# Gated cross-attention with a routed feed-forward: loads ordered by need, four small query groups, score chunks of 128 keys, normalisation spread over slots, the last two tiles multiplied by all experts

## The chip, the core and the metric

The kernel runs on one NeuronCore of a Trainium2 chip. The metric is the device time of one launch in microseconds (us), the median of three runs. The engines work beside each other: TensorE (PE) multiplies, VectorE (DVE) and ScalarE (ACT) read its PSUM results, GpSimd (POOL) works on SBUF only, SyncE (SP) starts transfers (DMA). They meet at semaphores. Every engine runs its own instructions strictly in the order in which they are written.

## The reference

```python
# x (8, 112, 256), ctx (8, 375, 192), 16 heads of 16
x = x + tanh(g_xattn) * xattn(layernorm(x), ctx, ctx, Wq, bq, Wk, bk, Wv, bv, Wo, bo)
x = x + tanh(g_ffn) * ffn(layernorm(x), wg, W, b)

def xattn(...):   # q = query @ Wq + bq, k = ctx @ Wk + bk, v = ctx @ Wv + bv
    return (softmax(q k^T / 4) v) @ Wo + bo          # for each of the 16 heads

def ffn(x, wg, W, b):                                # all 896 tokens, 8 experts
    probs = softmax(x @ wg); idx = argmax(probs)
    mask = one_hot(idx); loc = cumsum(mask) - mask   # place of a token with its expert
    mask = mask * (loc < 112)                        # C = 896 / 8
    return probs[idx] * (W[idx] @ x + b[idx])        # the expert's product, weighted
```

A token beyond its expert's 112 places gets nothing from the feed-forward. The kernel's gathered table has 112 rows for each expert (`CAP`).

## The kernel before

A tile is one batch element: 112 queries by 375 keys. Queries and keys are split into three bf16 parts, laid out by small transfers (`lay_q`, `lay_k`, issued by SP) in six rows per head dimension, so that one bf16 matmul per head gives a score in nearly full precision.

The work is written as a pipeline of slots. A loop over `s` runs on every engine, and each step of a tile has an offset: `at(s, OFFSET, n)` says which tile `b` does that step in slot `s`. A tile begins every 12 slots (`TURN`), so that each slot holds work of up to five tiles. The steps of a tile are, with their first offset in the code before:

- K steps (`project_k`, offsets -16 to -14) multiply keys; ACT makes `k_hi` and a copy (`k_copy`) of each half at -14 and -12; POOL splits the halves (`k_split`, three instructions) at -13 and -11; SP lays them out at -7.
- `scores` and `take_max` (0 to 11): one matmul per head into one of two PSUM banks (`sc`), and one DVE maximum over the 375 keys. A bank is used again when its maximum is taken.
- `split_max` (13) on POOL makes three bf16 parts of the 16 maxima, `turn_max` (14) on PE turns them, ACT copies them (`mrows`), SP lays them out (14 to 15, `MROW_AT`), so that the second score product subtracts the maximum.
- `scores_T` (17 to 28): the scores once more, transposed, four heads and one of three chunks of 125 keys each slot (`stp`); ACT takes the exponential (`prob`); `probs_v` (18 to 29) multiplies by the values, four heads in four strips of 32 columns.
- V steps (`project_v`, 12 to 16) make the values of the tile.
- `normalise_pv` (30) on DVE: transpose out of PSUM, reciprocal, product, transpose back; `through_wo` (31) on PE; `add_x` (32) on DVE with the statistics of the second layer norm.
- `rstd_2` and `normalise_2` (33) on POOL (the last two tiles' `normalise_2` on DVE), `turn_xn2` (35), `logits` (36).

So offset 35 of one tile, offset 11 of the tile two further and offset -13 of the tile four further are the same slot (35 = 12 x 3 - 1, and so on): each slot has a number from 0 to 11 in its turn of 12, and it is this number that counts for what meets on an engine. Within a slot the order is that of the loop's body. On POOL it is `split_max`, `k_split`, and then the second layer norm.

The first stage works on queries by groups (`QG`: tile 0, tiles 1 to 4, tiles 5 to 7). After the last slot comes the feed-forward. Tiles 0 to 6 are scattered by expert into a table in HBM (`scatter`, POOL), loaded again as eight blocks (`xin`), multiplied by their expert (`product`) and scattered to the output. Tile 7 is not scattered: it is multiplied by all eight experts (`dense`, 16 matmuls of 512 columns), and DVE adds the products by the token's share.

Of the kernel before, what the change touches and what calls it, by code (L numbers as in the profile page):

```python
# [22 lines left out]
NCH = 3  # L23
KN = NK // NCH
# [11 lines left out]
KR = 3  # L36
# [18 lines left out]
FIRST, LAST = -4, TURN * (B - 1) + LG_AT  # L55


QG = ((0, 1), (1, 5), (5, 8))

R0, R1, R2 = (0, 6), (6, 7), (7, 8)  # L60
ROUTE0_AT, PLACE0_AT, ASSIGN0_AT = 97, 98, 99
ROUTE1_AT, PLACE1_AT, ASSIGN1_AT = 109, 110, 111
SCAT0_AT = (100, 101, 102, 106, 107, 108)
# [20 lines left out]
def v_block(c, h):  # L84

    return (h, 24 + h, 16 + h if h < 8 else 32 + h)[c]


def build(nc, x, ctx, gx, gf, wq, bq, wk, bk, wv, bv, wo, bo, wg, wT, be, out):
# [3 lines left out]
    with ExitStack() as stack:  # L93
# [10 lines left out]
        bq_sb = sb("bq_sb", [128, 2])  # L104
        bk_sb = sb("bk_sb", [128, 2])
        bv_sb = sb("bv_sb", [128, 2])
# [7 lines left out]
        half = sb("half", [NQ, B])  # L114
# [21 lines left out]

        st1 = sb("st1", [NQ, B, 6])
        mv1 = sb("mv1", [NQ, B, 2])
        ve1 = sb("ve1", [NQ, B])
# [4 lines left out]
        k6_flat = sb("k6", [128, KR, H * NK], BF16)  # L144
        k6 = k6_flat[:, :, :].rearrange("p r (h n) -> p r h n", n=NK)
# [5 lines left out]
        prob = sb("prob", [128, 3, 4 * NQ])  # L151
        pvT = sb("pvT", [128, NQ * G])
# [6 lines left out]
        ve2 = sb("ve2", [NQ, B])  # L159
# [30 lines left out]
        s_x = [sem(f"x_of_group_{g}_loaded") for g in range(3)]  # L190
# [21 lines left out]
        s_qzero = [sem(f"zeros_in_q_{g}_ready") for g in range(3)]  # L212
# [5 lines left out]
        s_stat = sem("variance_ready")  # L218
        s_rstd = sem("rstd_ready")
# [8 lines left out]
        s_qlaid = [sem(f"q_rows_of_group_{g}_laid") for g in range(3)]  # L228
# [21 lines left out]
        s_x1 = sem("x1_ready")  # L250
        s_stat2 = sem("variance_2_ready")
# [12 lines left out]
        s_scat = sem("tokens_scattered")  # L264
        s_xin = [sem(f"expert_{e}_loaded") for e in range(E)]
# [8 lines left out]
        s_dense = sem("all_experts_product_in_psum")  # L274
        s_counted = sem("places_of_last_tile_taken")
# [4 lines left out]
        s_last = sem("last_tile_ready")  # L280
# [34 lines left out]
        def _(sp):  # L315
# [13 lines left out]
            def lay_k(b):  # L329
# [15 lines left out]
            sp.dma_start(wk_sb[:, :, :], wk).then_inc(s_wk, 16)  # L345
            load_ctx(0, 0, 1)
            sp.dma_start(x_sb[:, 1:5, :], x[:, 1:5, :]).then_inc(s_x[1], 16)
            load_ctx(1, 1, 2)
            sp.dma_start(x_sb[:, 5:B, :], x[:, 5:B, :]).then_inc(s_x[2], 16)
            lay_k(0)  # L350
            lay_q(0)
            for s in range(FIRST, LAST + 1):
                if s == 1:
                    lay_q(1)
                    load_ctx(2, 2, 5)
# [21 lines left out]
                if s == 93:  # L377
                    sp.wait_ge(s_x1, 6)
# [787 lines left out]
```

## Time and profile before

| what | value |
|---|---|
| runs | 225.04, 225.27, 226.06 us; median 225.27 |
| profiled execution | 226.61 us, of which the span from the first to the last instruction is 224.8 |
| PE busy | 184.9 us, 82% of the span, 1692 matmuls |
| DVE / ACT / POOL busy | 123.7 / 91.5 / 94.3 us |
| chain that ended last | PE 66%, DVE 13%, DMA 8%, POOL 5% |
| mean granted TensorE clock | 0.922 |
| HBM | read 10.03 MB, written 5.29 MB |

In the profile PE is a matmul's time and PEld a weight load's. The chain of waits is followed back from the last instruction: each piece is what released the one behind it, so pieces of PE there are times for which PE alone decided. Three stages can be told apart in it: 0 to 54.6 us, until the first transposed scores; 54.6 to 189.2 us, eight turns of 12 slots, some 18 us each where all steps are present; and 189.2 to 224.8 us, the rest of tile 7 and the experts.

### The profile page before, as it was taken

How to read it: one execution, taken by the hardware profiler on the slowest of the kernel's cores; microseconds unless marked ns; L12 is line 12 of the kernel's file. 1: busy time of each engine (PE TensorE's matmuls, PEld its weight loads, DVE VectorE, ACT ScalarE, POOL GpSimd, SP SyncE). 2: the span in 40 equal slices, each digit the busy share in tenths (PEclk: the TensorE clock that was granted, in tenths of full speed). 3: DMA queues.
4: the chain of work that ended last, by engine and by line, in shares of the span. 5: the costliest groups of instructions: out<-in, count | busy, mean ns of one | idle time of the engine just before them, and what ended most of it. 6: DMA issues, size and time to landing. Idle time of an engine off the chain costs nothing.

```text
span 224.8 us, 4335 instructions
## 1 busy us (share of the span) xinstructions
PE 184.9 (82%) x1692; PEld 111.7 (50%) x1692; DVE 123.7 (55%) x292; ACT 91.5 (41%) x200; POOL 94.3 (42%) x145
## 2 busy tenths in 40 slices
PE   0866869743999899899899989989989896479990
PEld 0342426412556466557556646646656563257640
DVE  7037465563454855754764675485585436254651
ACT  0262243231374365456527527544636654021200
POOL 5632639779245056038037235413022553103730
PEclk9999599995699999999999999999999998556998
DMA  6968049999940910840660490180351233560110
GB/s 187 264 156 169 0 107 291 226 238 294 291 139 16 224 65 5 191 109 3 142 162 0 100 203 3 40 171 0 94 146 57 69 113 116 155 175 28 57 51 20
DMA packets 17660, 27.40 MB, mean 122 GB/s; under 512 B 4007, under 2 KB 12817, under 8 KB 17272
## 3 DMA queue, kind: packets, MB, share of 16 engines
q1 hardware_dynamic: 15176, 23.82, 41.6%
q0 software_dynamic: 944, 2.28, 3.3%
q10 hardware_dynamic: 1520, 1.03, 1.9%
q8 instruction: 13, 0.21, 0.4%
q14 instruction: 7, 0.06, 0.1%
HBM read 10.03 MB, written 5.29 MB: 68 GB/s over the span
## 4 chain that ended last, share of the span: by engine, by line
PE 66%; DVE 13%; DMA 8%; POOL 5%; ACT 2%; issue 2%; ACTq 1%; SPq 1%; DVEq 0%
PE stp L476 14%; PE pv L491 12%; PE sc L465 8%; PE misc L522 4%; PE stp L407 4%; DMA bv_sb<-in_bv 4%; DVE nmax L809 4%; PE pj L423 3%; PE pj L439 3%; PE misc L580 2%; DVE pvT L816 2%; DMA k<-parts_k 2%; DMA q<-mrows 2%; PE pj L444 2%; PE pv L580 2%
## 5 line engine op out<-in xcount | busy, mean ns | idle before, releaser
L809 DVE TENSOR_REDUCE nmax<-sc 112x1 f32<-112x375 f32 x128 | 68.2, 543 | 54.6 <-PE sc L465 53.8
L733 ACT ACTIVATE prob<-stp 125x448 f32<-125x448 f32 x96 | 52.2, 544 | 61.2 <-PE stp L476 60.8
L465 PE MATMUL sc<-k,q 128*112 128x375 bf16 x128 | 41.8, 343 | 9.1 <-DVE nmax L809 6.7
L476 PE MATMUL stp<-q,k 128*125 128x112 bf16 x384 | 42.8, 236 | 3.2 <-DMA q<-mrows 3.2
L491 PE MATMUL pv<-prob,v_sb 125*32 125x112 f32 x768 | 38.7, 273 | 2.1 <-issue 1.3
L476 PEld LDWEIGHTS stp<-q,k 128*125 128x125 bf16 x384 | 30.3, 140 | 20.1 <-issue 16.5
L491 PEld LDWEIGHTS pv<-prob,v_sb 125*32 125x32 f32 x768 | 15.4, 108 | 23.6 <-ACT prob L733 10.1
L1000 POOL TENSOR_SCALAR ve<-mv 112x1 f32<-112x1 f32 x8 | 1.9, 233 | 57.4 <-DVE mv L838 57.4
L465 PEld LDWEIGHTS sc<-k,q 128*112 128x112 bf16 x128 | 17.2, 135 | 16.4 <-DVE nmax L809 11.4
L423 PE MATMUL pj<-ctx_sb,wk_sb 128*128 128x375 f32 x32 | 15.4, 580 | 7.8 <-DMA ctx_sb<-in_ctx 7.8
L1017 POOL TENSOR_TENSOR kf<-kf,parts_k 128x375 f32<-128x375 f32 x14 | 12.6, 899 | 19.1 <-ACT kf L677 19.1
L1011 POOL TENSOR_TENSOR parts_k<-kf,parts_k 128x375 bf16<-128x375 f32 x16 | 13.9, 875 | 5.1 <-ACT parts_k L665 4.0
L407 PE MATMUL stp<-early,wq_sb 128*128 128x112 f32 (+2 forms) x24 | 10.9, 615 | 2.8 <-ACT early L665 2.8
L671 ACT ACTIVATE parts_k<-pj,bk_sb 128x375 bf16<-128x375 f32 x16 | 9.0, 572 | 10.1 <-PE pj L428 8.2
L1117 POOL DMA_INDIRECT out<-res,ctx_sb x8 | 7.8, 974 | 12.4 <-DVE res L968 11.2
L423 PEld LDWEIGHTS pj<-ctx_sb,wk_sb 128*128 128x128 f32 x32 | 6.9, 235 | 9.6 <-issue 7.9
L522 PE MATMUL misc<-wo_sb,onorm 128*112 128x256 f32 x32 | 9.3, 418 | 2.3 <-DVE onorm L826 2.3
L1040 POOL DMA_INDIRECT slots<-rows,slot x7 | 7.1, 1016 | 8.2 <-DVE slot L888 6.8
L439 PE MATMUL pj<-wv_sb,ctx_sb 128*125 128x256 f32 x32 | 9.8, 389 | 0.7 <-ACT kf L677 0.7
L407 PEld LDWEIGHTS stp<-early,wq_sb 128*128 128x128 f32 x24 | 5.7, 282 | 6.5 <-issue 4.9
L428 PE MATMUL pj<-ctx_sb,wk_sb 64*128 64x375 f32 x32 | 8.3, 596 | 0.0
L677 ACT ACTIVATE kf<-pj,bk_sb 128x375 f32<-128x375 f32 x14 | 8.0, 572 | 0.0
(125 smaller groups left out, 240.7 us busy)
## 6 DMA issues: line engine op xcount, KB each, us to landing
k<-parts_k SPq DMA_DIRECT2D x48, 187.5 KB, 3.8
ctx_sb<-in_ctx SPq DMA_DIRECT2D x2, 1125.0 KB, 7.6
early<-in_wT SPq DMA_DIRECT2D x8, 256.0 KB, 4.3
slots<-empty SPq DMA_DIRECT2D x8, 224.9 KB, 4.6
ctx_sb<-slots SPq DMA_DIRECT2D x8, 224.9 KB, 4.5
q<-parts_q SPq DMA_DIRECT2D x6, 224.0 KB, 3.7
q<-parts_q SPq DMA_DIRECT2D x6, 168.0 KB, 3.7
k<-in_be SPq DMA_DIRECT2D x1, 896.0 KB, 5.1
```

The costliest lines, as they stand in the source:

```text
L407: mm = pe.matmul(stp[m][:, 0:(hi - lo) * NQ], wq_sb[:, c, m * 128:(m + 1) * 128], xnT[:, c, lo * NQ:hi * NQ], start=(c == 0), stop=(c == 1))
L423: pe.matmul(pj[n][:, 0:NK], wk_sb[:, 0, n * 128:(n + 1) * 128], ctx_sb[:, b, 0, :], start=True, stop=False)
L439: pe.matmul(pj[n][0:KN, 0:D], keys(n, slice(0, 128), 0), wv_sb[:, 0, :], start=True, stop=False)
L465: pe.matmul(sc[h % 2][0:NQ, 0:NK], q_heads(b)[:, h, :], k6[:, b % KR, h, :], start=True, stop=True).then_inc(s_sc, 1)
L476: mm = pe.matmul(stp[n % 2][0:KN, j * NQ:(j + 1) * NQ], k6[:, b % KR, h, c * KN:(c + 1) * KN], q_heads(b)[:, h, :], start=True, stop=True)
L491: mm = pe.matmul(pv[32 * j:32 * j + 32, g * NQ:(g + 1) * NQ], v_sb[0:KN, b % VR, v_block(c, 4 * g + j), :], prob[0:KN, n % 3, j * NQ:(j + ...
L522: mm = pe.matmul(misc[0:NQ, 0:D], onorm[:, g, :], wo_sb[:, g, :], start=(g == 0), stop=(g == 1))
L671: nc.scalar.activation(parts_k[:, b % 2, 0, m, :], pj[m][:, 0:NK], ACT.Identity, bias=bk_sb[:, m:m + 1]).then_inc(s_khi, 1)
L733: nc.scalar.activation(prob[0:KN, n % 3, :], stp[n % 2][0:KN, 0:4 * NQ], ACT.Exp, scale=SCALE).then_inc(s_p, 1)
L809: nc.vector.tensor_reduce(nmax[:, b % 2, h:h + 1], sc[h % 2][0:NQ, 0:NK], axis=AX.X, op=ALU.max, negate=True).then_inc(s_max, 1)
L1011: nc.gpsimd.tensor_tensor(parts_k[:, b % 2, 2, m, :], kf[:, b % 2, m, :], parts_k[:, b % 2, 1, m, :], ALU.subtract).then_inc(s_klo, 1)
L1017: nc.gpsimd.tensor_tensor(kf[:, b % 2, m, :], kf[:, b % 2, m, :], parts_k[:, b % 2, 0, m, :], ALU.subtract).then_inc(s_krest, 1)
```

## The change

- Loads: keys, values, biases (one packed array) and weights are asked for in the order of their use and from other queues; the context of tiles 2 to 4 is asked for by ACT, far earlier. A first activation loads the table ahead of its use.
- Query groups: tile 0, tiles 1 and 2, tiles 3 to 5, tiles 6 and 7. The K steps of tile 1 move ahead of the slots, and POOL's constants behind the splits of tile 1 and of group 1. The slots begin at 0.
- The score chunks have 128, 128 and 119 keys. `scores_T` loads 128 columns of weights for every chunk; for the last these go past the tile's end by 9 columns, whose results are not read.
- `normalise_pv` is cut into `turn_pv`, `divide` and `turn_back` in slots 30, 31 and 32, with the maxima of these slots between them. `through_wo` moves to 33, `add_x` to 34, `rstd_2` and `normalise_2` to 35, `turn_xn2` to 37, `logits` to 38. `split_max` moves forward to 12, `turn_max` to 13. `turn_xn2` shares a PSUM bank with the maxima and now waits for `mrows` of the tile two further.
- Tiles 6 and 7 are both multiplied by all experts (`dense(t, p)`), and six tiles are scattered. The dense products of tile 6 are written between the last steps of tile 7 on PE.

```diff
-V_EARLY = -10
-SPLITMAX_AT, MAXT_AT, MROW_AT = 13, 14, 15
+V_EARLY = -11
+SPLITMAX_AT, MAXT_AT, MROW_AT = 12, 13, 14
 T_AT, PV_AT = 17, 18
-NORM_AT, WO_AT, ADD_AT = 30, 31, 32
-LN_AT, X2T_AT, LG_AT = 33, 35, 36
+NORM_AT, WO_AT, ADD_AT = (30, 31, 32), 33, 34
+LN_AT, X2T_AT, LG_AT = 35, 37, 38
-QG = ((0, 1), (1, 5), (5, 8))
+QG = ((0, 1), (1, 3), (3, 6), (6, 8))
...
-                    mm = pe.matmul(stp[n % 2][0:KN, j * NQ:(j + 1) * NQ],
-                                   k6[:, b % KR, h, c * KN:(c + 1) * KN], q_heads(b)[:, h, :],
+                    k0 = h * NK + CHUNKS[c][0]
+                    mm = pe.matmul(stp[n % 2][:, j * NQ:(j + 1) * NQ],
+                                   k6_flat[:, b % KR, k0:k0 + 128], q_heads(b)[:, h, :],
...
             def turn_xn2(b):
                 pe.wait_ge(s_xn2, b + 1)
+                pe.wait_ge(s_mrows, min(b + 3, B))
...
+            turn_share(0)
+            dense(0, 0)
+            through_wo(B - 1)
+            choose_bias(0)
+            dense(0, 1)
+            turn_xn2(B - 1)
             turn_xin(0)
-            places(2, *R2)
-            for e in range(1, E):
+            logits(B - 1)
+            dense(0, 2)
+            places(2, B - 1, B)
+            dense(0, 3)
+            turn_xin(1)
...
+            for p in range(4):
+                dense(1, p)
...
-                if found := at(s, NORM_AT, 1):
-                    normalise_pv(found[0])
+                if found := at(s, NORM_AT[0], 1):
+                    turn_pv(found[0])
+                if found := at(s, NORM_AT[1], 1):
+                    divide(found[0])
+                if found := at(s, NORM_AT[2], 1):
+                    turn_back(found[0])
...
+            for m in range(2):
+                k_split(1, m)
+            rstd(3)
+            for m in range(2):
+                q_lo(1, m)
+            ones_in_k(2)
+            zeros_in_q(2)
+            zeros_in_q(3)
```

The tables of offsets do not show what meets on an engine. On POOL, in a turn with all steps (`kf` and `parts_k` are the key split, `ve`, `rs` and `rows` the second layer norm, `mparts` the parts of the maxima), before:

```order
L1000 TENSOR_SCALAR ve<-mv 112x1
L1001 TENSOR_TENSOR rs<-ve,half 112x1
L1006 TENSOR_SCALAR rows<-rows,mv,rs 112x256
L1017 TENSOR_TENSOR kf<-kf,parts_k 128x375
L1020 CAST parts_k<-kf 128x375
L1011 TENSOR_TENSOR parts_k<-kf,parts_k 128x375
L1033 CAST mparts<-nmax 112x16
L1034 TENSOR_TENSOR mrest<-nmax,mparts 112x16
```

The same place on POOL in the changed kernel:

```order
L1105 TENSOR_TENSOR parts_k<-kf,parts_k 128x375
L1094 TENSOR_SCALAR ve<-mv 112x1
L1095 TENSOR_TENSOR rs<-ve,half 112x1
L1100 TENSOR_SCALAR rows<-rows,mv,rs 112x256
L1127 CAST mparts<-nmax 112x16
L1128 TENSOR_TENSOR mrest<-nmax,mparts 112x16
```

The layer norm (three instructions) stood ahead of the first key split, and now stands between it and the parts of the maxima.

On PE, from the last K step of a tile (its second half, `pj<-ctx_sb,wk_sb` twice) to the turn of the maxima (`misc<-ident_b,mparts`), before:

```order
L428 MATMUL pj<-ctx_sb,wk_sb 128x375 x2
L491 MATMUL pv<-prob,v_sb 32x112 x4
...
L439 MATMUL pj<-wv_sb,ctx_sb 125x256
L491 MATMUL pv<-prob,v_sb 32x112 x4
L476 MATMUL stp<-q,k 125x112 x4
L465 MATMUL sc<-k,q 112x375
L444 MATMUL pj<-wv_sb,ctx_sb 125x256 x2
L515 MATMUL misc<-ident_b,mparts 48x112
L491 MATMUL pv<-prob,v_sb 32x112 x4
```

and in the changed kernel, the end of the same stretch:

```order
L449 MATMUL pj<-wv_sb,ctx_sb 128x256
L528 MATMUL misc<-ident_b,mparts 48x112
L546 MATMUL misc<-ident,rows 128x112 x2
L503 MATMUL pv<-prob,v_sb 32x112 x4
L487 MATMUL stp<-q,k 128x112 x4
L475 MATMUL sc<-k,q 112x375
L454 MATMUL pj<-wv_sb,ctx_sb 128x256 x2
```

The turn of the maxima has moved ahead of a `pv` product, a `stp` group, a score and the two V products of 256 columns, and the turn of the normalised rows (`misc<-ident,rows`) now stands right behind it.

On DVE, the normalisation and the maxima around it, before:

```order
L809 TENSOR_REDUCE nmax<-sc 112x1 x13
L816 STREAM_TRANSPOSE pvT<-pv 128x448
L818 RECIPROCAL rden<-pvT 128x14
L819 TENSOR_TENSOR onT<-pvT,rden 128x2x7x16
L826 STREAM_TRANSPOSE onorm<-onT 128x224
L809 TENSOR_REDUCE nmax<-sc 112x1 x3
```

and in the changed kernel:

```order
L881 STREAM_TRANSPOSE pvT<-pv 128x448
L883 RECIPROCAL rden<-pvT 128x14
L874 TENSOR_REDUCE nmax<-sc 112x1 x2
L886 TENSOR_TENSOR onT<-pvT,rden 128x2x7x16
L874 TENSOR_REDUCE nmax<-sc 112x1
L895 STREAM_TRANSPOSE onorm<-onT 128x224
L874 TENSOR_REDUCE nmax<-sc 112x1 x3
```

Three maxima have moved in between the four instructions of the normalisation.

## Rows read from the trace of the kernel before

**Rows 1.** The page: busy time and share of each engine.

```profile
PE 184.9 (82%) x1692; PEld 111.7 (50%) x1692; DVE 123.7 (55%) x292; ACT 91.5 (41%) x200; POOL 94.3 (42%) x145
```

**Rows 2.** Windows, one turn: length, busy by engine, PEclk, DMA share, GB/s.

```profile
94.00:112.00 18.00, 17.01 (x196) 10.47 (x195) 10.99 (x24) 9.76 (x21) 7.26 (x13) 1.00 0.40 93
```

**Rows 3.** Chain of waits, one turn: start us, us, what.

```profile
109.21 0.55 DVE nmax L809
...
111.95 0.37 PE sc L465
...
117.18 0.83 PE pj L428 x4
118.01 0.33 PE pv L491 x8
118.34 0.37 PE stp L476 x4
118.70 0.16 PE sc L465
...
119.92 0.43 PE pj L439 x2
```

**Rows 4.** Timeline, same turn: start us, us, engine, line, operation, [idle before].

```profile
114.47 0.23 POOL L1000 TENSOR_SCALAR ve<-mv 112x1 f32<-112x1 f32 x1 [7.74 <-DVE mv L838]
115.47 1.23 POOL L1006 TENSOR_SCALAR rows<-rows,mv,rs 112x256 f32<-112x256 f32 x1
...
118.51 0.57 ACT L677 ACTIVATE kf<-pj,bk_sb 128x375 f32<-128x375 f32 x1
119.16 0.90 POOL L1017 TENSOR_TENSOR kf<-kf,parts_k 128x375 f32<-128x375 f32 x1 [2.46 <-ACT kf L677]
121.50 0.20 POOL L1033 CAST mparts<-nmax 112x16 bf16<-112x16 f32 x1
122.34 0.22 POOL L1036 TENSOR_TENSOR mparts<-mrest,mparts 112x16 bf16<-112x16 f32 x1
123.52 0.23 PE L515 MATMUL misc<-ident_b,mparts 112*48 112x112 bf16 x1
123.79 0.26 ACT L665 ACTIVATE mrows<-misc 48x112 bf16<-48x112 f32 x1 [0.41 <-PE misc L515]
```

**Rows 5.** Timeline, weight loads of one group of four transposed score matmuls.

```profile
181.66 0.31 PEld L476 LDWEIGHTS stp<-q,k 128*125 128x125 bf16 x4 [0.17 <-issue]
```

**Rows 6.** Chain of waits, first stage.

```profile
23.26 6.17 PE stp L407 x8
29.63 1.00 DVE nmax L809 x2
...
40.07 0.87 POOL kf L1017
...
42.74 4.59 DMA k<-parts_k
...
50.06 4.51 DMA q<-mrows
```

**Rows 7.** Windows of PE (last numbers: PEclk, DMA share, GB/s), and chain.

```profile
56.00:60.00 4.00, 4.00 (x31) 0.52 1.07 260
...
57.33 0.61 PE stp L476 x4
...
58.79 0.61 PE stp L476 x4
```

**Rows 8.** Chain of waits, last stage; last row from the timeline.

```profile
189.30 0.66 DVE pvT L816
...
191.16 2.06 PE misc L522 x4
...
212.09 1.72 PE pj L560 x4
...
220.89 0.32 SPq L387 DMA_DIRECT2D out<-last  x1
```

More of the change, by code:

```diff
@@ L433, in keys @@
                 def keys(c, rows_in, part):
-                    return ctx_sb[rows_in, b, part, c * KN:(c + 1) * KN]
+                    k0, kn = CHUNKS[c]
+                    return ctx_sb[rows_in, b, part, k0:k0 + kn]
+                half = D // 2
+                kn = CHUNKS[2][1]
                 if n < 2:
@@ L438, in project_v @@
                     pe.wait_ge(s_kf, 2 * (newest - 1) + n + 1)
-                    pe.matmul(pj[n][0:KN, 0:D], keys(n, slice(0, 128), 0), wv_sb[:, 0, :],
+                    pe.matmul(pj[n][:, half:half + D], keys(n, slice(0, 128), 0), wv_sb[:, 0, :],
                               start=True, stop=False)
@@ L443, in project_v @@
                         rows_in = slice(c * REST, (c + 1) * REST)
-                        pe.matmul(pj[c][0:KN, 0:D], keys(c, rows_in, 1), wv_sb[rows_in, 1, :],
+                        pe.matmul(pj[c][:, half:half + D], keys(c, rows_in, 1), wv_sb[rows_in, 1, :],
                                   start=False, stop=True, tile_position=(c * REST, 0))
@@ L447, in project_v @@
                     for c in range(2):
-                        pe.matmul(pj[c][0:KN, D:D + 128], keys(2, slice(0, 128), 0),
-                                  wv_sb[:, 0, c * 128:(c + 1) * 128], start=True, stop=False)
+                        pe.matmul(pj[c][0:kn, 0:half], keys(2, slice(0, 128), 0),
+                                  wv_sb[:, 0, c * half:(c + 1) * half], start=True, stop=False)
                 if n == 4:
@@ L452, in project_v @@
                         rows_in = slice(c * REST, (c + 1) * REST)
-                        pe.matmul(pj[c][0:KN, D:D + 128], keys(2, rows_in, 1),
-                                  wv_sb[rows_in, 1, c * 128:(c + 1) * 128], start=False, stop=True,
+                        pe.matmul(pj[c][0:kn, 0:half], keys(2, rows_in, 1),
+                                  wv_sb[rows_in, 1, c * half:(c + 1) * half], start=False, stop=True,
                                   tile_position=(c * REST, 0)).then_inc(s_v, 1)
@@ L970, in _ @@
                                                ALU.mult, ALU.add).then_inc(s_res, 1)
-            dve.wait_ge(s_share, 1)
-            dve.wait_ge(s_beT, 1)
-            link(nc.vector.tensor_tensor(last[:, :], pv[0:NQ, 0:D], rows[:, b, X1:X1 + D], ALU.add))
-            banks = (pj[0], pj[1], stp[0], stp[1])
-            for e in range(E):
-                if e % 2 == 0:
-                    dve.wait_ge(s_dense, e // 2 + 1)
-                ins = nc.vector.scalar_tensor_tensor(
-                    last[:, :], banks[e // 2][0:NQ, (e % 2) * D:(e % 2 + 1) * D], share[:, e:e + 1],
-                    last[:, :], ALU.mult, ALU.add)
-                if e < E - 1:
-                    link(ins)
-                else:
-                    ins.then_inc(s_last, 1)
+                if e == 3:
+                    take_bias(1)
+            for p in range(4):
+                add_dense(1, p)
         @block.gpsimd
@@ L1079, in more_constants @@
                     .then_inc(s_eno, 1)
[L1081 to L1085 removed]
+            for s in range(END):
                 if found := at(s, SPLITMAX_AT, 1):
```

473 lines of the change are left out of this document (268 added, 205 removed).

## The prediction

> **What bounds the kernel now.** I read the page first: PE is busy for 184.9 of 224.8 us, the next engine for 124 [rows 1]. Then the windows of one turn of 12 slots: 17.01 of 18.00 us are PE's, at the full clock of 2.4 GHz, while DVE has 11, ACT 10 and POOL 7 [rows 2]. So in the middle of the program PE decides, and a cut in its work or in its waits counts in full. Then the chain of waits in such a turn: the only pieces there that aren't PE's lie between 109.21 and 111.95 us, where PE waits for DVE, which does a whole normalisation ahead of a maximum [rows 3]. Last I looked at what is late without deciding: POOL finishes the parts of the maxima at 122.56, and PE asks for them at 123.52, 0.96 us later [rows 4]. The changed order is read against this margin.
>
> The sum goes by the profiled execution, 226.61 us with a span of 224.8; the median of the runs is 225.27. The difference that I forecast is added to the median.
>
> **Loads, groups, first stage.** Before, the first maximum starts at 29.63, behind a 6.17 us product for a group of four tiles [rows 6]; with two tiles it is half. In the new order DVE does the statistics of tiles 6 and 7 and two query rests ahead of the first maximum, and these wait for the smaller product; stepping the new order through with the old durations gives about 27.2. The keys of tile 1 were split late, at 40.07, behind POOL's constants, and landed at 47.33 [rows 6]; now they are there before they are asked for. What is late next is the turn of tile 0's maxima. The twelve slots between took 17.7 us (29.63 to 47.33), some 3.4 of it waits that go (keys of tile 1, context of tile 2), and get about 1 of new query work: 15. The key split of tile 2 and the parts of the maxima follow on POOL, so that the max rows are asked for near 47, not 50.06. Their transfer took 4.51 beside a load of 1.1 MB [rows 6], which is over by then; with 3.4 the transposed scores start at 50.3, not 54.6. Taken: **-4.3**; bounds 0 (another wait in the place of that for the keys) and -7.3 (the whole of 47.33 to 54.6).
>
> **Normalisation.** Before, the score behind it starts at 111.95. Now `pv` needs only the first transpose, done at about 110.35; with a `pv` product (0.33) and a `stp` group (0.37) the score stands at 111.06, and it then takes 0.16, not 0.37 [rows 3]. That is 1.05 a turn, for six turns with scores beside it, and 0.5 for tile 6: **-6.8**. Bounds 0 and -9.4: of the 2.74 us up to 111.95, two `stp` groups, two scores and a `pv` product are work, 1.39, and the other 1.35 would go in seven turns. Moving `through_wo` by two slots keeps its wait at nothing.
>
> **The turn of the maxima.** Here the change costs. Two moves meet. PE asks a slot earlier, and on POOL the layer norm now stands between the key split and the parts of the maxima, because offsets 35 and -13 share a slot and the loop writes the split first; `split_max` at 12 comes behind both. From the end of the last K step on PE (118.01): ACT's copy is done at 119.08, POOL's split runs from 119.16 to 121.50, 2.34; the layer norm takes 2.23 (114.47 to 116.70); the parts 1.06 (121.50 to 122.56) [rows 3, 4]. In sum 1.15 + 2.34 + 2.23 + 1.06 + 0.05 = 6.83 us. PE's own work in that time is 0.33; then 0.37 + 0.16 + 0.33; then 0.37 + 0.43 + 2 x 0.16 + 0.33; then 0.37 + 0.16 + 0.43: 3.60 [rows 3], or 3.3 with the shorter groups below. PE waits 3.5 us, and nothing passes it. Behind `turn_max` stands `turn_xn2`, which now waits until ACT has copied the maxima: 123.52 to 124.05 [rows 4], 0.4 beyond the matmul itself. That is 3.9 a turn where K steps and layer norm both occur: slots 35, 47, 59, 71, four turns, 15.6. The turn before has the key split alone (4.6 - 3.3 = 1.3), the two behind the layer norm alone (0.7 and 1.2 by the same steps, from `add_x`). Together **+18.8**; bounds +8 (were the layer norm free) and +22.
>
> **Chunks of 128 keys.** 96 groups of four. A group takes 0.37 [rows 3]; its four loads of 125 bf16 columns take 0.31 with about 0.057 between starts [rows 5]. A score of 375 columns takes 0.16 behind a load of 112 columns, so 112 columns stream in 0.048, and four in 0.19. So the load, not the stream, sets the group. No row shows a bf16 load of 128 columns. Bounds: no gain, or a loss of 3 columns in 125 (+0.01 a group), and 0.18 gained, when only the stream is left. The third chunk moves no result: the same count of columns. I take the middle, 0.09, as nothing in the rows favours an end: 96 x 0.09 = **-8.6**.
>
> The Trainium skill has a rule here ("TensorE: Matmul & The Clock Gate", section on Fast Weight Load): a non-fp32 load of exactly 128 columns is split in four parallel chunks, four times as fast in theory and about twice as measured. With loads at half their time the group would fall by some 0.07 to 0.09, with a quarter by up to the bound; no row of this trace shows it, since its 128-column loads are all fp32.
>
> **The clock.** A wait of 3.5 us is long enough for the clock to matter. Before, PE stands for most of the 4.51 us in which the max rows land (until 54.6) [rows 6]; in 56 to 60 it is granted 0.52, and a slot takes 1.46 (57.33 to 58.79) [rows 7], where the same slot takes 0.86 at the full clock [rows 3]. 0.52 is nearly all of the window at the 1.2 GHz level, so the low level lasts some 5.3 us past the restart there and costs 5.3 x (1 - 0.86 / 1.46) = 2.2. With part of it inside the wait I take 1.8 for each of the four long waits: **+7.2**; bounds 0 and +12 (the short ones too).
>
> **The end.** From the last transposed product to the end it is 35.5 us now. There DVE's normalisation runs from 189.30, and the product through `wo` takes 2.06, at half the clock [rows 8]. Now two of four parts of tile 6's dense product, 1.72 each [rows 8], lie in the waits of tile 7's chain, and six scatters instead of seven bring the expert blocks earlier. Stepping through the new order at the full clock, tile 7's logits come at 6.5, the first expert product at 11.7, the eighth at 20.4, tile 7's dense products at 27.3, the last issue at 28.4, and 3.9 to the end [the last issue is at 220.89, rows 8]: 32.4, 3.1 less. If the clock falls as before, a dense part of 3.4 us stands ahead of `wo`: +3. Half of that: **-1.6**; bounds -4 and +2.
>
> Sum: -4.3 - 6.8 + 18.8 - 8.6 + 7.2 - 1.6 = **+4.7**. The profiled execution would take 231.3, the median 230.0.
>
> **Rivals.**
> (a) *The loads nearly vanish.* By the same rule at its fullest a group takes 0.19: 8.6 more is gained, and 1.4 of it lost again in longer waits (POOL's path doesn't shrink): 222.8, faster. For: four loads fill 0.31 of 0.37. Against: the first load of each group stays exposed behind `pv`. 0.12.
> (b) *The clock holds.* PE works densely around the waits, and each may be too short. Then 230.0 - 7.2 = 222.8, faster. For: it held through 1.35 us of idling a turn [rows 2, 3]. Against: the idling ahead of 54.6 is of the same length, and there the level was low. 0.15.
> (c) *128 columns load as 125 do.* +8.6 and the waits shorter by 1.4: 237.2, slower. 0.08.
> (d) *The first stage gains nothing*, since transfers or POOL's constants hold the max rows: 234.3. For: the DMA engines are full in much of that stage. 0.12.
> (e) *The POOL path is shorter than I say*, because PE's slots are longer than I add up (the waits that I left out stand on its side), so that the wait is 1.5 us, not 3.5: 4 x 2.0 less, 222. 0.05.
> My forecast, wait of 3 to 4 us and low clock behind it: 0.48, alone 226 to 235.
>
> Within 0.5% (224.1 to 226.4) no difference can be told from none. From the cases: faster, most of (a), (b), (e) and a sliver of the forecast, 0.27; same 0.10; slower 0.63. Range 220.5 to 237.
>
> **What would show it.** In the changed profile the trace must have PE waiting for POOL's `mparts` for about 3.5 us ahead of L528 in four turns, POOL going from `rows` L1100 straight to `mparts`, and turns of 20 to 22 us there, against under 17 where neither K steps nor layer norm meet. The 128-column loads show their price in the length of a `stp` group: 0.28 by my sum, 0.19 by (a), 0.38 by (c). PEclk shows 5s behind each wait, or not (b). The first transposed scores near 50.3, and the last stage near 33 to 34 us. The forecast is wrong if these waits are under 2 us, or if PE keeps its clock.

## The result

| | before | changed |
|---|---|---|
| runs, median (lowest to highest) | 225.36 us (225.04 to 226.06) | 256.62 us (256.1 to 258.94) |
| span of the profiled execution | 224.8 | 254.8 |
| mean granted TensorE clock | 0.922 | 0.886 |

The ratio is 1.140, 95% interval 1.133 to 1.148. Some executions of a kernel take over 1.5% longer than its fastest, and the ratios here leave these out. Forecast were 230.0 us and a range up to 237: the direction was right, the size far off. In a later comparison the changed kernel took 260.04 us (258.61 to 261.44) beside 228.48, ratio 1.143 (1.131 to 1.155):

> The changed kernel once more, beside the others on the same chip: 1.12 to 1.145 of the kernel before.

Three points in both traces place the 30.0 us. The first transposed scores start at 59.56, not 54.61: +5.0. From there to the last `pvT` transpose it is 160.8 us (to 220.38), not 134.7 (to 189.30): +26.1. The last stage has 34.4, not 35.5: -1.1.

One part of this differs from execution to execution. In the profiled one of the later comparison (span 258.4) tile 7's slots, from 207 on, take 17.4 us, not 13.4, and the rest is within 0.5 us of the above.

### The profile page after: what moved, and what is told of

Same layout as the page of the kernel before. It is cut to its first block, busy times and chain, and to the rows that moved or that the text cites. A ratio compares the mean times of both kernels' runs of the same rounds, so it can differ in the third digit from the quotient of the medians.

```text
span 254.8 us, 4453 instructions
## 1 busy us (share of the span) xinstructions
PE 196.3 (77%) x1719; PEld 113.2 (44%) x1719; DVE 137.6 (54%) x301; ACT 92.5 (36%) x208; POOL 96.0 (38%) x164
## 4 chain that ended last, share of the span: by engine, by line
PE 50%; POOL 19%; DVE 17%; issue 5%; ACT 4%; DMA 3%; POOLq 0%; DVEq 0%
PE stp L487 7%; PE pv L503 7%; PE sc L475 7%; DVE early L854 4%; DVE nmax L874 4%; PE pj L583 3%; PE pj L454 3%; PE pj L430 3%; POOL rows L1100 3%; POOL kf L1111 3%; POOL parts_k L1105 3%; PE misc L538 2%; PE misc L555 2%; PE pj L435 2%; PE pj L458 2%
## 5 line engine op out<-in xcount | busy, mean ns | idle before, releaser
L790 ACT ACTIVATE prob<-stp 128x448 f32<-128x448 f32 (+1 forms) x96 | 52.0, 544 | 54.5 <-PE stp L487 53.4
L503 PE MATMUL pv<-prob,v_sb 128*32 128x112 f32 (+1 forms) x768 | 41.0, 289 | 1.9 <-issue 1.4
L487 PE MATMUL stp<-q,k 128*128 128x112 bf16 x384 | 38.8, 229 | 0.2 <-DMA q<-mrows 0.2
L487 PEld LDWEIGHTS stp<-q,k 128*128 128x128 bf16 x384 | 22.3, 104 | 18.9 <-issue 18.3
L503 PEld LDWEIGHTS pv<-prob,v_sb 128*32 128x32 f32 (+1 forms) x768 | 16.1, 113 | 24.2 <-issue 9.4
L854 DVE TENSOR_SCALAR early<-x_sb,mv,rs 112x256 f32<-112x256 f32 x8 | 13.5, 1728 | 5.0 <-POOL rs L1089 5.0
L528 PE MATMUL misc<-ident_b,mparts 112*48 112x112 bf16 x8 | 1.9, 240 | 17.4 <-POOL mparts L1130 17.4
L583 PE MATMUL pj<-early,x2T 128*112 128x512 f32 x24 | 13.1, 682 | 0.5 <-DVE q L981 0.5
L713 ACT ACTIVATE parts_k<-pj,bqkv_sb 128x375 bf16<-128x375 f32 x16 | 9.0, 572 | 6.6 <-PE pj L435 6.6
L449 PE MATMUL pj<-wv_sb,ctx_sb 128*128 128x256 f32 x32 | 11.1, 431 | 0.1
L1119 POOL TENSOR_TENSOR parts_q<-early,parts_q 128x224 bf16<-128x224 f32 (+2 forms) x8 | 5.6, 715 | 14.7 <-ACT parts_q L707 14.7
L528 PEld LDWEIGHTS misc<-ident_b,mparts 112*48 112x48 bf16 x8 | 0.8, 101 | 20.5 <-POOL mparts L1130 20.5
```

Source lines behind the costliest of these rows:

```text
L449: pe.matmul(pj[n][:, half:half + D], keys(n, slice(0, 128), 0), wv_sb[:, 0, :], start=True, stop=False)
L487: mm = pe.matmul(stp[n % 2][:, j * NQ:(j + 1) * NQ], k6_flat[:, b % KR, k0:k0 + 128], q_heads(b)[:, h, :], start=True, stop=True)
L503: mm = pe.matmul(pv[32 * j:32 * j + 32, g * NQ:(g + 1) * NQ], v_sb[0:kn, b % VR, v_block(c, 4 * g + j), :], prob[0:kn, n % 3, j * NQ:(j + ...
L583: mm = pe.matmul(bank[0:NQ, 0:2 * D], x2T[:, (GATHERED + t) % 2, c, :], wT_sb[:, 2 * p:2 * p + 2, c, :], start=(c == 0), stop=(c == 1))
L713: nc.scalar.activation(parts_k[:, b % 2, 0, m, :], pj[m][:, 0:NK], ACT.Identity, bias=bk_sb[:, m:m + 1]).then_inc(s_khi, 1)
L790: nc.scalar.activation(prob[0:kn, n % 3, :], stp[n % 2][0:kn, 0:4 * NQ], ACT.Exp, scale=SCALE).then_inc(s_p, 1)
```

## The profile after

The page of the changed kernel, the row that answers to [rows 1], and the granted clock in 40 slices:

```profile
PE 196.3 (77%) x1719; PEld 113.2 (44%) x1719; DVE 137.6 (54%) x301; ACT 92.5 (36%) x208; POOL 96.0 (38%) x164
PEclk9999558995999965997699679959999999589999
```

PE is busy for 11 us more. The dense products of tile 6 are new work, 4 x 1.72 us [rows 8], and the shorter `stp` groups take about as much away, so most of the 11 is slower work. The clock row says where: between slices 15 and 27 (89 to 172 us) it dips once a turn.

**The first stage.** Timeline of the changed kernel around the first maximum:

```profile
25.86 1.98 POOL L1119 TENSOR_TENSOR parts_q<-early,parts_q 128x224 bf16<-128x224 f32 x2
25.92 8.61 DVE L854 TENSOR_SCALAR early<-x_sb,mv,rs 112x256 f32<-112x256 f32 x2 [1.48 <-POOL rs L1089]
27.78 2.67 POOL L1147 MEMSET k<- 128x1000 f32 x3
30.40 3.99 POOL L1152 MEMSET q<- 128x896 f32 x5
34.33 1.69 POOL L1172 MEMSET v_sb<- 128x1536 f32 x1
34.63 0.99 DVE L874 TENSOR_REDUCE nmax<-sc 112x1 f32<-112x375 f32 x2
35.22 0.56 PE L475 MATMUL sc<-k,q 128*112 128x375 bf16 x1 [7.64 <-DVE nmax L874]
```

Two instructions of DVE, the normalisation of tiles 6 and 7, take 8.61 us. Apart, the first takes 1.45 beside POOL's `q_lo`, the second 7.23: it starts before the memset of `k` and ends with the last memset of `q`. The first maximum, forecast at 27.2, starts at 34.63, and PE stands 7.64 us for it. DVE's own idle time ahead of the pair is 1.48; the rest is in the length of the instruction, so it is held off while it runs.

**A turn of 12 slots.** Timeline of one turn, which answers to [rows 4]:

```profile
135.42 0.90 POOL L1111 TENSOR_TENSOR kf<-kf,parts_k 128x375 f32<-128x375 f32 x1 [16.10 <-ACT kf L719]
136.96 0.85 POOL L1105 TENSOR_TENSOR parts_k<-kf,parts_k 128x375 bf16<-128x375 f32 x1
138.76 1.23 POOL L1100 TENSOR_SCALAR rows<-rows,mv,rs 112x256 f32<-112x256 f32 x1
140.79 0.22 POOL L1130 TENSOR_TENSOR mparts<-mrest,mparts 112x16 bf16<-112x16 f32 x1
141.06 0.23 PE L528 MATMUL misc<-ident_b,mparts 112*48 112x112 bf16 x1 [3.10 <-POOL mparts L1130]
141.33 0.26 ACT L707 ACTIVATE mrows<-misc 48x112 bf16<-48x112 f32 x1 [3.66 <-PE misc L528]
141.73 0.38 PE L546 MATMUL misc<-ident,rows 112*128 112x112 f32 x2 [0.44 <-ACT mrows L707]
```

This is the forecast path, POOL going from the key split through the layer norm to the parts of the maxima, and the forecast wait: 3.10 us, and 3.10 to 3.12 in four turns. Then 0.44 more for ACT's copy. Windows of the same turn (columns as in [rows 2]), of a stretch behind the wait, and of one ahead of its end:

```profile
126.94:150.93 23.99, 20.09 (x197) 11.63 (x195) 10.96 (x24) 9.81 (x22) 7.22 (x13) 0.86 0.30 71
142.34:149.16 6.82, 6.82 (x51) 4.36 (x47) 1.69 (x4) 1.79 (x5) 0.93 (x2) 0.50 0.02 4
136.00:141.00 5.00, 1.94 (x18) 0.79 (x16) 1.54 (x3) 1.67 (x4) 4.43 (x11) 1.00 0.00 0
```

The turn takes 24.0 us, where [rows 2] had 18. PE works 1.94 of the 5 us up to 141 at the full level, and from 142.34 on 6.82 us without a gap at 0.50, 1.2 GHz: its densest work falls where it is slowest. The four turns with K steps and layer norm take 24.7, 24.0, 24.0, 24.0, not 18.16 each: +24.1 of the 26.1 us.

**The last slots.** Timeline, tile 7's slots; the last two rows are PE's wait for the normalised rows of tile 6:

```profile
213.21 0.94 POOL L1134 DMA_INDIRECT slots<-rows,slot  x1 [0.30 <-issue]
214.53 0.57 POOL L1095 TENSOR_TENSOR rs<-ve,half 112x1 f32<-112x1 f32 x1
215.14 0.41 DVE L911 TENSOR_SCALAR rows<-rows,mv,rs 112x256 f32<-112x256 f32 x1 [3.23 <-POOL rs L1095]
215.61 0.41 PE L546 MATMUL misc<-ident,rows 112*128 112x112 f32 x2 [2.30 <-DVE rows L911]
```

Five of six scatters stand ahead of `rstd_2` of tile 6. This wait of 2.30 us is not in the forecast.

The 17.4 us that the same slots take in the later comparison have another reason. There ACT stands for 3.85 us ahead of an exponential, though its input was there at 212.81, and PE stands with it (`remote` and `issue`: the profile shows no instruction that was waited for):

```profile
215.90 0.54 ACT L790 ACTIVATE prob<-stp 119x448 f32<-119x448 f32 x1 [3.85 <-remote]
216.50 0.60 PE L503 MATMUL pv<-prob,v_sb 119*32 119x112 f32 x8 [3.69 <-issue]
```

The profiled executions of e1, e5, e8 and e10 below have the same stop of 3.8 us at this exponential and e2 has one of 2.4; the first one of the changed kernel and those of e3, e6, e9 and e11 have none. What ACT waits for is open. These slots take 13.4 to 17.7 us in all these executions, so turns say more than whole times.

For the last stage, windows of the kernel before and of the changed one, from the last `pvT` to the end:

```profile
189.30:224.80 35.50, 24.18 (x85) 14.91 (x85) 16.65 (x46) 3.74 (x12) 8.75 (x11) 0.74 0.28 81
```

```profile
220.38:254.80 34.42, 28.64 (x104) 15.45 (x104) 20.57 (x55) 3.93 (x13) 8.61 (x10) 0.94 0.27 76
```

PE has 4.5 us more to do, at a better clock; the chain ends with two stretches of `dense` of tile 7, 3.4 us each.

## The experiments

The theory after the comparison: three causes. POOL's memsets hold off DVE's normalise (first stage); the wait of 3.1 us in four turns; and the low clock that it sets off, which costs as much again. The rivals are given with each. Beside these runs the kernel before took 228 us in the median (223.9 to 230.9 over all), so each ratio is to executions of it taken beside that run. `pvT` to `pvT` is a turn.

**e1, order on POOL.**

```diff
+                if found := at(s, LN_AT, 1):
+                    rstd_2(found[0])
+                    if found[0] < GATHERED:
+                        normalise_2(found[0])
                 for m in range(2):
                     if (found := at(s, KSPLIT_AT[m], 1)) and found[0] > 1:
                         k_split(found[0], m)
...
-                if found := at(s, LN_AT, 1):
-                    rstd_2(found[0])
-                    if found[0] < GATHERED:
-                        normalise_2(found[0])
```

> The changed kernel with one edit: on POOL the second layer norm of a slot is written ahead of the key split, as it was before the change. Theory W (PE's wait for the parts of the maxima, and the low clock behind it, are the loss in the middle): the layer norm has its input some 1.7 us before the key split has, so about 2 us leave POOL's path; the wait of 3.1 us ahead of L528 in four turns falls to about 1, the 6.83 us at the low level behind each of them go (3.4 us a turn by half the clock), turns fall from 24.0 to 18.5, and the time from 256.6 to about 235. Theory W2 (the wait matters, the clock falls all the same): only 4 x 2 us, about 248. Rival (the turns are long for a reason that is not this wait): no change, 255 to 258.

Measured: 255.74 us (249.61, 255.27, 256.20 and 256.43) beside 228.3; no ratio is given. In the profiled execution, that of 256.20, the wait at L528 fell from 3.10 to 1.60 in the four turns, and the turns only to 23.70. Windows of one turn of it, and of the stretch behind its wait:

```profile
124.82:148.52 23.70, 21.30 (x197) 12.14 (x195) 10.96 (x24) 9.92 (x22) 7.20 (x13) 0.78 0.32 73
137.79:148.03 10.24, 9.92 (x75) 6.02 (x79) 2.25 (x5) 3.21 (x8) 1.80 (x3) 0.50 0.12 32
```

The low level lasts 10.24 us here, not 6.8, and 1.2 of the 1.5 us won came back as slow work. W, 235 us, is out. In this execution halving the wait bought almost nothing. That can't be said of the one of 249.61 us, which is near W2's 248; its mean clock was 0.881, not 0.851, and it has no trace.

**e8, the wait filled with work.**

```diff
+                if 2 <= b <= 5:
+                    pe.wait_ge(s_x1, b - 1)
+                    for _ in range(7):
+                        pe.matmul(misc[0:NQ, 0:D], wo_sb[:, 0, 0:NQ], wv_sb[:, 0, :], start=True, stop=True)
                 pe.wait_ge(s_mp, b + 1)
```

> The changed kernel as it is, with seven further fp32 products of 256 columns on PE ahead of the turn of the maxima for tiles 2 to 5, written to misc and read by nobody: 14 passes of 0.22 us, 3.08 us, put into the wait of 3.1 us. Nothing else moves; POOL's path is as long as before. Theory K (PE idles, and so the clock falls, and the low clock costs as much as the wait): the clock stays at the full level in these four turns, which fall from 24.0 to 20.6: 256.6 - 4 x 3.4 = 243, though PE does more work. Rival H (the level does not depend on that wait): the products come on top or change nothing, 256 or more, and the level is low for 6.8 us a turn as before.

Measured: 247.79 us (245.9 to 248.35), ratio 1.084 (1.076 to 1.093), where the changed kernel has 1.14. Windows of a turn, and the products in the timeline of the turn ahead of it:

```profile
121.50:142.55 21.05, 20.18 (x211) 12.34 (x209) 10.94 (x24) 9.80 (x22) 7.21 (x13) 1.00 0.33 81
111.28 3.19 PE L523 MATMUL misc<-wv_sb,wo_sb 128*112 128x256 f32 x14
114.56 0.23 PE L532 MATMUL misc<-ident_b,mparts 112*48 112x112 bf16 x1
```

The kernel does seven products more in each of four turns and is 9 to 12 us faster. POOL's path is as before: the turn of the maxima (here L532) starts 14.22 us behind `pvT` in this turn, as in the changed kernel. PE is busy meanwhile (14 passes in 3.19 us), and the level is full from 65.07 to 205.01. Only what stands behind the wait got shorter. So the low level costs 24.0 - 21.05 = 2.9 us a turn, 3.6 in the first of the four: 12.4 in all. Theory K is shown, rival H is out.

**e10, a later turn with the layer norm in the way; e5, both moves undone.**

```diff
-SPLITMAX_AT, MAXT_AT, MROW_AT = 12, 13, 14
+SPLITMAX_AT, MAXT_AT, MROW_AT = 13, 14, 15
-LN_AT, X2T_AT, LG_AT = 35, 37, 38
+LN_AT, X2T_AT, LG_AT = 35, 38, 39
```

> The changed kernel with the parts, the turn and the layout of the maxima at 13, 14, 15 again (turn_xn2 and logits at 38 and 39), but with the layer norm still behind the key split on POOL. Separates the two moves that met: 1.9 us of PE work come ahead of L528, the path on POOL keeps its 2.2 us. PE's wait falls from 3.1 to about 1.2. If a wait of that size still sets off the low level (1.6 us did in e1): turns of 22 to 23.5 and 250 us or so. If the level holds: turns of 24.0 - 1.9 - 3.4 = 18.8 to 19.2, 236 us. Either way the time lies between that of e1 and of e5.

> The changed kernel with the order on POOL of e1_pool_order, and with the parts of the maxima, their turn and their layout at offsets 13, 14, 15 again (turn_xn2 and logits one slot later, 38 and 39). e1 left a wait of 1.6 us, and the low level behind it grew to 10.24 us a turn, so that the turn only fell from 24.0 to 23.7. Theory K (any wait of that length there sets off the low level, and that is what costs): a slot more of PE work (a pv product, a stp group, a score and two V products, 1.9 us) covers the 1.6 us; no wait, full clock, and the turn is that of before, 18.16, less 1.05 for the normalisation and 0.64 for the loads (what the before-kernel with 128-column loads gained a turn): 16.5; the time falls by 4 x 7.2 us to 227 to 230. Rival H (PE's clock falls in these turns for another reason, such as the denser work): turns stay at 22 to 24, time at 250 or more.

Measured: e10 247.47 us (245.88 to 248.07), ratio 1.087 (1.076 to 1.098); e5, with e1's order as well, 233.49 us (232.37 to 234.72), ratio 1.026 (1.019 to 1.034). Windows of the four turns of e10:

```profile
78.09:97.57 19.48, 16.98 (x197) 9.92 (x195) 10.95 (x24) 9.82 (x22) 7.25 (x13) 1.00 0.38 89
97.57:118.59 21.02, 18.52 (x197) 11.16 (x195) 10.95 (x24) 9.81 (x22) 7.25 (x13) 0.92 0.35 81
118.59:141.14 22.55, 20.07 (x196) 11.83 (x194) 11.04 (x25) 10.04 (x22) 7.24 (x13) 0.82 0.38 90
141.14:162.48 21.34, 19.20 (x200) 11.51 (x198) 10.96 (x24) 9.71 (x21) 7.23 (x13) 0.87 0.29 66
```

The wait at L528 is 1.68 to 1.71 us in all four turns (1.2 was expected), and the clock answers differently: no fall in the first turn, 3.41 us at the low level in the second, 10.24 in the third, 3.41 in the fourth. With the same wait the turn costs 19.5, 21.0, 22.5 or 21.3. In e5 the wait is 0.17 to 0.20, the clock is full from 62.67 to 188.97, and the four turns take 17.94 to 17.97. That is K once more, but not the 16.5 expected (nor the 227 to 230 us): e5 has hardly a wait and no low clock there, and gained only 0.2 on the 18.16 of before. With the loads (0.63, e4) and the spread (0.69, e7) it should be 16.84; 1.1 us a turn was still missing (e9).

**e2 and e11, the first stage.** POOL waits until xn is written, ahead of `q_lo` (e2), or behind it (e11):

```diff
             rstd(3)
+            pool.wait_ge(s_xn, B)
             for m in range(2):
                 q_lo(1, m)
             ones_in_k(2)
```

```diff
             for m in range(2):
                 q_lo(1, m)
+            pool.wait_ge(s_xn, B)
             ones_in_k(2)
```

> The changed kernel with one more wait: POOL starts its q_lo of group 1 and its memsets (k, q, v_sb) only when DVE has written all eight tiles of xn. Theory C (DVE's two-input-free SBUF-to-SBUF normalise and POOL's work in SBUF hold each other up: 8.61 us for two instructions at 25.92): the two take about 0.41 us each, the first maximum starts near 27.5 instead of 34.63, and since POOL's constants start 1 us later only, the first transposed scores come about 4 to 7 us earlier than 59.56: 250 to 252. Rival D (the 8.61 us are a wait for something else, such as the loads that land at that time): the two instructions stay near 8 us and POOL's constants come 8 us later: 257 or more.

> The changed kernel with POOL's wait for xn between its q_lo of group 1 and its memsets, not ahead of both. In the changed kernel the first of the pair of DVE's normalise (25.92) took 1.45 us beside q_lo, the second 7.23 us beside the memsets of k and q, and ended with the last of them. Theory C1 (the memsets hold DVE's instruction off, q_lo only slows it): the pair takes some 1.9 us and ends near 27.9, the first maximum comes near 28.2, 0.8 us behind e2's, the first transposed scores near 53.3. Theory C2 (any work of POOL in SBUF that follows without a gap does it): the second instruction starts behind q_lo all the same, and the result is as C1 or up to 0.5 us later. Rival D (something else held DVE until 34.5): the pair still takes over 6 us and the memsets start behind it, at 34 or later. Time of the run by C1: 2 to 5 us below the changed kernel's, ratio 1.12 to 1.135.

Measured: e2 254.86 us (252.73 to 257.7), ratio 1.131 (1.107 to 1.155); e11 253.86 us (253.42 to 254.58), ratio 1.129 (1.117 to 1.140). Timelines of e2 and then of e11:

```profile
25.82 0.73 DVE L854 TENSOR_SCALAR early<-x_sb,mv,rs 112x256 f32<-112x256 f32 x2 [1.49 <-POOL rs L1089]
27.75 2.67 POOL L1147 MEMSET k<- 128x1000 f32 x3
52.48 0.56 PE L487 MATMUL stp<-q,k 128*128 128x112 bf16 x4 [0.31 <-DMA q<-mrows]
```

```profile
25.80 1.30 DVE L854 TENSOR_SCALAR early<-x_sb,mv,rs 112x256 f32<-112x256 f32 x2 [1.48 <-POOL rs L1089]
```

The same two instructions take 0.73 us, or 1.30 beside `q_lo`, not 8.61, and the memsets start no later. The first maximum comes at 27.43 (e11: 28.21), and the first transposed scores at 52.48 (52.79). 7.1 us of the first stage were this. That the memsets held the instruction is shown; D is out. C2, that a run of any other POOL work would do the same, was not separated: in e11 only two `q_lo` instructions follow each other there. The whole time shows less than the trace. For e2 250 to 252 was expected, and both intervals overlap the 1.133 to 1.148 of the changed kernel, so a gain in the whole time, of some 1%, is not clear of noise. In e2 2.9 of the 7.1 us go in tile 7's slots (16.3, not 13.4), where ACT stops for 2.4 us and, from 207.14, the level is low for 13.65 us.

**e3, scatters.**

```diff
-SCAT_AT = (102, 103, 104, 105, 106, 107)
+SCAT_AT = (102, 103, 104, 108, 109, 110)
```

> The changed kernel with three of the six scatters written behind rstd_2 of tile 6 on POOL. Theory T (the scatters of 0.95 us and 1.25 from start to start stand ahead of rstd_2(6), whose input is there at 211.9 and which starts at 214.17, and PE waits 2.3 us for it at L546): rstd_2 starts near 212.2, PE's wait of 2.30 us goes, and the clock may hold at 217.43; the time falls by 2 to 4 us, 253 to 254.5. Rival: the feed-forward waits for the scatters instead (expert blocks land later): no change, or 1 us more.

Measured: 259.47 us (256.77 to 260.5), ratio 1.143 (1.119 to 1.168). PE's wait of 2.30 us at L546 is gone (its weight load waits 0.26), but there is no gain in the time: in this execution the clock fell at 204.98 for 10.24 us, ahead of the place that was changed. That the scatters made the wait is shown, its worth is not; the 253 to 254.5 us expected did not come.

**e4, the kernel before with loads of 128 columns.**

```diff
-        k6_flat = sb("k6", [128, KR, H * NK], BF16)
+        k6_flat = sb("k6", [128, KR, H * NK + 16], BF16)
...
-                    mm = pe.matmul(stp[n % 2][0:KN, j * NQ:(j + 1) * NQ],
-                                   k6[:, b % KR, h, c * KN:(c + 1) * KN], q_heads(b)[:, h, :],
+                    k0 = h * NK + c * KN
+                    mm = pe.matmul(stp[n % 2][:, j * NQ:(j + 1) * NQ],
+                                   k6_flat[:, b % KR, k0:k0 + 128], q_heads(b)[:, h, :],
```

> The kernel before with one edit: each weight load of scores_T takes 128 columns of keys instead of 125, the three further columns give rows of PSUM that nobody reads. This prices the load alone. If a load of 128 bf16 columns is the faster kind: each of 96 groups of four takes 0.28 us or less instead of 0.37, and the time falls by up to 8 us if PE decides in every slot, to 217 to 220; it falls by less where ACT's exponentials (0.54 a slot) or DVE's maxima decide. If it costs as 125 columns do: 225 to 226, no change.

Measured: 222.17 us (221.18 to 222.73), ratio 0.983 (0.968 to 0.998). Timeline of one group (compare [rows 5]) and windows of a turn of e4:

```profile
109.32 0.21 PEld L477 LDWEIGHTS stp<-q,k 128*128 128x128 bf16 x4 [0.17 <-issue]
```

```profile
105.64:123.17 17.53, 16.47 (x197) 9.83 (x195) 11.15 (x25) 9.64 (x22) 7.26 (x13) 1.00 0.43 99
```

Four loads of three columns more take 0.21 us, not 0.31. In the chain a group takes 0.30, not 0.37. The turn falls by 0.63. The Trainium skill ("TensorE: Matmul & The Clock Gate", section on Fast Weight Load) has such loads at about half the time as measured; here it is two thirds for the load and four fifths for the group. Its fourfold speed in theory stands there for fp8, with two bf16 elements to a read, so it is no price for this bf16 load, as the prediction takes it.

**e6, all three causes mended; e7, the normalisation in one slot; e9, turn_xn2 ahead.** e6 is e5 with e2's wait and e3's table. e7 changes the first line of e6, e9 the others:

```diff
-NORM_AT, WO_AT, ADD_AT = (30, 31, 32), 33, 34
+NORM_AT, WO_AT, ADD_AT = (30, 30, 30), 33, 34
-LN_AT, X2T_AT, LG_AT = 35, 38, 39
+LN_AT, X2T_AT, LG_AT = 35, 36, 37
-                pe.wait_ge(s_mrows, min(b + 3, B))
+                pe.wait_ge(s_mrows, min(b + 2, B))
-                    pe.wait_ge(s_x1, b - 1)
+                    pe.wait_ge(s_lge, b - 1)
```

> e5_late_turn, with POOL's wait for xn ahead of its memsets (e2_memsets_wait, 7 us earlier to the first transposed scores) and three scatters behind rstd_2 of tile 6 (e3_tail). If the three causes add up: first transposed scores at about 52, seven turns of 16.5 and the last stage of 33 to 36: 218 to 222, a few per cent below the kernel before. Rival: the gain of the first stage is taken back by a low clock somewhere later, as 3.3 of 7.1 us were in e2: 222 to 226.

> e6_combined with the three parts of the normalisation in one slot again (30, 30, 30), all else the same. Prices the spread alone, where no wait and no low clock covers it. By the sum of the prediction each turn gets 1.05 us longer, 7 to 8 us in all. Rival: PE's wait for the whole normalisation (1.35 us a turn) is long enough to set off the low level, and it costs more, 3 us a turn or over; or DVE's work is hidden, and it costs nothing.

> e6_combined with turn_xn2 and logits at offsets 36 and 37, ahead of the turn of the maxima in a turn as they stood before the change, so that turn_xn2 waits for max rows that are long there, and turn_max waits for the logits of the tile two behind. e6's turns were 17.97, where 18.16 - 0.64 (loads) - 0.70 (spread) = 16.8 was to be had. Theory M (the missing 1.15 is the meeting in PSUM: L528, ACT's copy, L546 stand in a row, 0.44 of it PE's wait for the copy, and L546 and the logits stand on the far side of POOL's path, where nothing covers them): the turn falls to 16.9 to 17.3, the time by 5 to 7 us to 218 to 220. Rival P (POOL's path from add_x through the layer norm and the key split to the parts of the maxima sets the turn): PE only waits longer at L528 instead, 17.9 a turn, no gain, and perhaps a wait long enough for the low level.

Measured: e6 224.61 us (222.53 to 224.95), ratio 0.986 (0.980 to 0.992); e7 227.59 us (226.16 to 231.16), ratio 0.998 (0.994 to 1.001); e9 220.70 us (219.42 to 221.32), ratio 0.968 (0.959 to 0.977). e6 was expected at 218 to 222 us and turns of 16.5, e7 at 7 to 8 us above e6, e9 at 218 to 220. Windows of a full turn of e6, e7 and e9, in this order:

```profile
106.44:124.41 17.97, 16.98 (x197) 9.91 (x195) 10.96 (x24) 9.81 (x22) 7.22 (x13) 1.00 0.42 96
```

```profile
110.09:128.75 18.66, 16.98 (x197) 9.91 (x195) 11.13 (x24) 9.80 (x22) 7.20 (x13) 1.00 0.40 92
```

```profile
106.11:123.00 16.89, 16.55 (x197) 9.97 (x195) 10.96 (x24) 9.69 (x22) 7.22 (x13) 1.00 0.44 102
```

With the three causes mended the change is worth 1.4%. Its spread normalisation is worth 0.69 us a turn (18.66 to 17.97) at a full clock in both, so the wait for the whole normalisation does not set off the low level (PE idles 1.68 us a turn in e7, 0.83 of it in that wait, and 0.99 in e6). e9 finds the missing piece: in e6 the turn of the maxima, ACT's copy and `turn_xn2` stand in a row at POOL's late end; with `turn_xn2` ahead nothing waits at L528 (0.2 in e6), the turn is 1.08 shorter, theory M holds and P is out. e9 is 3.2% faster than the kernel before and has the lowest time of all versions, though its interval overlaps that of e4 (0.968 to 0.998).

## Why the prediction was wrong

| step of the sum | forecast | measured | from |
|---|---|---|---|
| loads, groups, first stage | -4.3 | +5.0 | both traces; -2.1 without the memsets (e2) |
| normalisation spread, a turn | -1.05 | -0.69 | e6, e7 |
| wait for `mparts`, each of four turns | 3.5 | 3.1 | the trace after |
| the same, the turn ahead and two behind | 1.3, 0.7, 1.2 | 0.9, 0.4, 0.7 | the trace after |
| `turn_xn2` behind it, a turn | 0.4 | 1.1 | e6, e9 |
| chunks of 128, a turn | -1.08 | -0.63 | e4 |
| low clock, four turns together | +7.2 | +12.4 | e8 |
| the end | -1.6 | -1.1 | both traces |

- **The step that failed in its mechanism is the first: "Loads, groups, first stage".** It was stepped through "with the old durations", and one old duration did not hold. Before, POOL's memsets ran beside maxima that DVE reads from PSUM, and nobody was held up. The change moved them beside a DVE instruction that reads and writes SBUF, and that one took 7.2 us in place of 0.4. Nothing in the sum asked what an engine does beside its new neighbour. The bounds (0 and -7.3) left out a loss. 9.3 of the 25.3 us by which the profiled sum missed are here, 7.1 of them shown by e2. The other 2.2 are the max rows: in e2 they are asked for at 50.41, not near 47, and land in 2.02 us, not 3.4. Rival (d) had POOL's constants in it, but as what holds the max rows, not DVE. What a rule would have said: the Trainium skill ("SBUF — State Buffer", section "Who interferes with whom") states that VectorE and GpSimd share a pair of SBUF ports, that a `tensor_scalar` can take both, and that the one that comes second is blocked. The trace agrees as far as it goes, though it doesn't show how the instruction used the ports, and is worse than the rule: the instruction started at 27.30 beside a `q_lo`, and waited through eight memsets, not through one instruction.
- **With this step right the time would still lie outside the range.** Without the memsets the kernel still takes 253.9 to 254.9 us, above 237 (e2, e11). The four turns cost 24.1 us, where the sum has 4 x (3.9 + 1.8 - 1.05 - 1.08) = 14.3: 9.8 of the 25.3, and the largest part of that is the clock, 5.2. The slots and turns around them have 5.7 (+2.0, not -3.7), the end 0.5.
- **"The turn of the maxima" was right in mechanism, place and size:** 3.10 to 3.12 us ahead of L528 in four turns, POOL going from `rows` straight to `mparts`. Its tail was mis-sized. `turn_xn2` was priced at 0.4 for the copy; that it and the logits now stand where no work of POOL's path covers them makes it 1.1. It is by this wait that the forecast of a slower kernel came true, not by luck.
- **"The clock" was right in kind and mis-sized:** 1.8 a wait forecast, 2.9 to 3.6 measured, and the 12.4 in all lie above its bound of 12. The price of a us at the low level was about right (2.2 for 5.3, 0.42; here 2.9 for 6.83, 0.43). What failed is the length: 5.3 us were read off the first stage [rows 6, 7] and cut down for a part inside the wait; here three stretches of 6.83 us lie wholly behind the wait, and of the first, 10.24, all but 1.2. Rival (b) is out: the trace shows that the clock falls, e8 what it costs. Rival (e) is out with the wait of 3.1.
- **"Chunks of 128 keys":** the middle of the bounds was too much. The group takes 0.30 with the load at 0.21, not 0.28; in a turn 0.63 comes out of 12 groups, not 0.84; PE is busy for 0.70 less (17.17 before, 16.47 in e4) and idles 0.07 more, and the rest was not followed. Rivals (a) and (c) are both out.
- **"Normalisation":** 0.69 a turn, not 1.05. The 1.35 us that the prediction calls waiting are too many: the trace before has PE waiting 0.77 us for the maximum behind the normalisation (0.83 in e7, none in e6) and 0.23 ahead of a `pv` product, and that one stays in e6. PE's work is the same in e6 and e7, 16.98.
- **Not in the sum:** tile 7's slots take 13.4 us (207.00 to 220.38), not 11.6. Spread over slots, the normalisation and layer norm of tile 6 come so late that scatters and then PE's last slots meet them. e3 removes the wait of 2.30, and e6 and e9 still have 13.4 and 14.2 there, and other executions 16 to 17.7, so the rest of it is open.
- **The end:** -1.1 by another road. Forecast were 32.4 us at a full clock; it took 34.4 at 0.94, where the kernel before had 35.5 at 0.74. The products for tile 6 cost PE 4.5 us that the better clock covers. No run separates the two.

What the measured terms leave: 5.0 + 24.1 + 2.0 (the other turns and slots) - 1.1 = 30.0. The 24.1 of the four turns are, each, -0.69 - 0.63 + 3.1 + 1.1 + 2.9 to 3.6 = 5.8 to 6.5, where 5.8 to 6.5 were measured.

## What to carry to other kernels

Where a change moves instructions of one engine, look not only at who waits for whom, but at what each moved instruction now runs beside: eight POOL memsets beside a DVE instruction in SBUF cost 7 us of the first stage here, and one wait on POOL gave them back there. When PE gets a wait, its price is the wait and the slow work behind it, and halving the wait may win little (1.6 and 1.7 us still set off the low level in seven of eight turns of e1 and e10); take it away whole, by more work of PE ahead of it or by a shorter path. Price the parts one at a time on the kernel that stands: here a good part (128-column loads, 1.7% with an interval of 0.2 to 3.2%, one edit) was buried under two moves that met in a slot.

## What the runs showed of the hardware

- A DVE `tensor_scalar` of 112x256 fp32 in SBUF, one of two that take 0.73 us together in e2, took 7.23 us beside eight POOL memsets that followed each other without a gap; DVE's maxima from PSUM took 0.55 us beside the same memsets.
- A bf16 weight load of 128 columns is shorter than one of 125: four take 0.21 us (e4) and 0.31 us (the kernel before).
- Waits of 3.1 us set off 6.83 to 10.24 us at the low level each time, in the four turns of all five profiled executions that have them. With waits of 1.7 us the level stayed, or fell for 3.41 or 10.24 us, within one execution (e10); with 1.6 it fell for 10.24 us four times (e1). With 0.2 us at most at that place (e5, e6, e9), and with 1.68 us of idling a turn in e7 (0.83 us the longest wait), it held for 119 to 133 us on end.
- Seven useless products in each of four turns, put into a wait of 3.1 us, made a kernel 9 to 12 us faster (e8).
- ACT stood for 3.8 us ahead of one exponential in tile 7's slots in five profiled executions, and not in others, one of them of the same kernel; nothing in the profile shows why.
